# Expert FFN with routed tokens on one core: token ids stand behind the y rows in DRAM instead of in a tensor of their own

## What is computed

```python
def _L0_cond_ref(x, w, b):
    y = jax.lax.conv_general_dilated(x, w, window_strides=(1,), padding=[(K - 1, 0)], feature_group_count=D, ...)
    return y + b

def _L0_ffn_ref(x, w_router, w_experts):
    logits = jnp.einsum('bsh,eh->bse', x, w_router)
    idx = jnp.argmax(logits, axis=-1)
    all_out = jnp.einsum('bsh,efh->bsef', x, w_experts)
    out = jnp.take_along_axis(all_out, idx[:, :, None, None], axis=2)[:, :, 0, :]
    return out
x = x + _L0_ffn_ref(_L0_cond_ref(x, cond_2048[:, None, :], L0_cond_b), L0_ffn_w_router, L0_ffn_w_experts)
```

## Time and profile before

| | |
|---|---|
| median of 3 runs | 599.31 us |
| the profiled execution | 599.66 us |
| its span | 598.0 us |
| PE busy | 546.1 us (91%) |
| DVE busy | 348.2 us (58%) |
| ACT busy | 192.9 us (32%) |
| POOL busy | 221.2 us (37%) |
| mean granted TensorE clock | 0.957 |
| HBM read, written | 93.45 MB, 40.52 MB |

### The profile page before, as it was taken

One profiled execution on the slowest core, in us unless ns is written; L12 is line 12 of the kernel. 1 busy time (PEld: TensorE's weight loads), 2 busy tenths in 40 slices (PEclk: granted clock), 3 DMA queues, 4 the chain that ended last, 5 costly groups with the idle time before them and its releaser, 6 DMA issues.

```text
span 598.0 us, 10202 instructions
## 1 busy us (share of the span) xinstructions
PE 546.1 (91%) x3151; PEld 456.9 (76%) x3152; DVE 348.2 (58%) x404; ACT 192.9 (32%) x361; POOL 221.2 (37%) x222
## 2 busy tenths in 40 slices
PE   9999997789799987999899999999999999999930
PEld 7988886669688765788778888888888888888830
DVE  7999999449079561243887433275348332755720
ACT  7764654425390000012545110051015100514200
POOL 1300898765637722332222233321432242324321
PEclk9999999869999989799989999999999999999975
DMA  8734738626888359454998956368558754795451
GB/s 349 277 111 151 266 122 272 237 73 251 285 258 329 95 175 360 169 159 157 329 379 273 317 176 198 118 224 303 176 172 289 242 175 141 221 305 176 130 186 36
DMA packets 54936, 129.44 MB, mean 216 GB/s; under 512 B 7936, under 2 KB 29056, under 8 KB 54656
## 3 DMA queue, kind: packets, MB, share of 16 engines
q0 software_dynamic: 17616, 55.10, 26.3%
q1 hardware_dynamic: 15840, 54.42, 25.9%
q10 hardware_dynamic: 21456, 19.60, 12.0%
HBM read 93.45 MB, written 40.52 MB: 224 GB/s over the span
## 4 chain that ended last, share of the span: by engine, by line
PE 53%; DMA 4%; issue 2%; DVE 1%; ACT 1%; ACTq 1%; POOL 0%; POOLq 0%; DVEq 0%
PE ps L1099 53%; DMA out<-x_row,ids_first 2%; DMA x_row<-x_rows,idx 2%; ACT w_sb L522 1%; DMA out<-x_row,idx 1%; DVE w_sb L842 0%; ACTq L364 0%; POOL x_row L1183 0%; DVE x_row L870 0%; DVE ys L862 0%; DVE y_cols L857 0%; POOLq L1208 0%; DVEq L879 0%; DMA idx_in_sb<-id_sorted 0%; POOL idx L1214 0%
## 5 line engine op out<-in xcount | busy, mean ns | idle before, releaser
L1099 PE MATMUL ps<-w_sb,ys 128*128 128x512 f32 x1680 | 388.9, 394 | 11.2 <-DVE ys L862 6.3
L1099 PEld LDWEIGHTS ps<-w_sb,ys 128*128 128x128 f32 x1680 | 318.9, 190 | 80.1 <-issue 10.3
L857 DVE STREAM_TRANSPOSE y_cols<-y_blk 128x1024 f32<-128x1024 f32 x37 | 46.0, 1244 | 165.1 <-PE ps L1099 141.1
L541 ACT CAST ys<-y_cols 128x1024 fp32r<-128x1024 f32 x37 | 39.1, 1057 | 284.1 <-DVE y_cols L857 258.9
L684 DVE SCALAR_TENSOR_TENSOR y_pre<-x_all,cst,y_pre 128x1024 f32<-128x1024 f32 x72 | 87.3, 1288 | 0.1
L975 PE MATMUL ps<-x_all,bands 128*128 128x128 f32 x640 | 78.2, 279 | 4.0 <-issue 3.9
L975 PEld LDWEIGHTS ps<-x_all,bands 128*128 128x128 f32 x640 | 74.0, 193 | 7.5 <-issue 7.4
L842 DVE TENSOR_TENSOR w_sb<-w_raw,w_sb 128x1024 fp32r<-128x1024 f32 x56 | 64.2, 1220 | 20.2 <-ACT w_sb L522 17.3
L1190 POOL DMA_INDIRECT out<-x_row,idx x32 | 37.6, 1175 | 86.4 <-DVE x_row L870 80.9
L1214 POOL COPY idx<-idx_in_sb 128x1 int32<-128x1 int32 x34 | 9.3, 273 | 147.5 <-DMA out<-x_row,idx 136.4
L522 ACT CAST w_sb<-w_raw 128x1024 fp32r<-128x1024 f32 x56 | 53.9, 1048 | 21.5 <-PE ps L1099 15.5
(11 more groups left out here) (130 smaller groups left out, 208.7 us busy)
## 6 DMA issues: line engine op xcount, KB each, us to landing
w_raw<-experts SPq DMA_DIRECT2D x56, 512.0 KB
y_blk<-y_sorted ACTq DMA_DIRECT2D x148, 128.0 KB
x_all<-x_t SPq DMA_DIRECT2D x32, 520.0 KB, 6.0
w_lead<-experts SPq DMA_DIRECT2D x8, 512.0 KB
bands<-conv_full SPq DMA_DIRECT2D x2, 1024.0 KB, 10.9
y_blk<-y_sorted SPq DMA_DIRECT2D x8, 128.0 KB
idx_in_sb<-id_sorted POOLq DMA_DIRECT2D x36, 1.0 KB
x_row<-x_rows,idx POOLq DMA_INDIRECT x34
```

What stands on the lines that cost most here:

```text
L541: nc.scalar.copy(ys[:, HI, k, :, :].rearrange("p c s -> p (c s)"), y_cols[k][:, :, :].rearrange("p c s -> p (c s)")).then_inc(ys_hi, 1)
L857: V.transpose(y_cols[k][:, :, :].rearrange("p m (t i) -> p t m i", t=4), y_blk[:, k, :, :, :]).then_inc(y_blocks, 1)
L1099: mm = nc.tensor.matmul(out_ps[k][:, f * HALF:(f + 1) * HALF], ys[:, a, k, c, :], w_sb[:, (b * HC + c) * H + f * HALF:(b * HC + c) * H + ( ...
```

## The change

The tensor `id_sorted` is gone. A row of `y_sorted` has 1040 instead of 1024 elements (`ROW`), 4160 B: the 16 behind the row of y (`ID_COPIES`) hold the token's id. The staging buffers have the same rows, 512 B more per partition each. POOL writes the ids of a group into the staging buffer with one copy (`write_ids`), and the scatter of rows carries them along. The scatters of ids, `find_rest`, `fill_rest` and `fill_ids` are gone. Instead POOL writes 128 empty rows with the id `NO_TOKEN` to the start of each expert's part before the first group is scattered (`empty_rows`, eight direct DMAs out of one row per partition in `rows_odd`); the tokens' rows are then written over them. Waits on `id_out` become waits on `y_out`.

```diff
-        y_sorted = nc.dram_tensor("y_sorted", [EXPERTS * TOKENS, H], F32, kind="Internal").ap()
-        id_sorted = nc.dram_tensor("id_sorted", [ROWS, ID_STEP], I32, kind="Internal").ap()
+        y_sorted = nc.dram_tensor("y_sorted", [ROWS, ROW], F32, kind="Internal").ap()
...
                 if g == 1 and n == g * HC:
 
                     act.wait_ge(before_ready, 1)
+                    act.wait_ge(no_token_out, EXPERTS * 16)
...
             act.wait_ge(first_table, 1)
             act.wait_ge(y_out[1], 2 * TPG * 16)
-            act.wait_ge(rest_out, 32)
...
             low_y(1, 1)
-            find_rest()
             count_slots()
...
-            G.memset(no_token[:, :], NO_TOKEN).then_inc(no_token_ready, 1)
-            G.memset(token[:, TILES:], 0).then_inc(token_ready, 1)
-            G.tensor_copy(token[:, 0:TILES], const(C_TOKEN, TILES)).then_inc(token_ready, 1)
+            G.memset(empty_row[:, 0:H], 0.0).then_inc(no_token_ready, 1)
+            G.memset(empty_row[:, H:].bitcast(I32), NO_TOKEN).then_inc(no_token_ready, 1)
+            G.tensor_copy(token[:, :], const(C_TOKEN, TILES)).then_inc(token_ready, 1)
...
                 pool.wait_ge(turn_copied, (g + 1) * HC * 2)
                 pool.sem_inc(dma_allowed, 1)
+                pool.wait_ge(ids_written, g + 1)
...
+            def write_ids(g):
+
+                if g == 0:
+                    pool.wait_ge(token_ready, 1)
+                elif g == 1:
+
+                    pool.wait_ge(no_token_out, EXPERTS * 16)
+                else:
+
+                    pool.wait_ge(y_out[g % 2], TPG * 16)
                 pool.sem_inc(dma_allowed, 1)
...
+                ids = token[:, g * TPG:(g + 1) * TPG].unsqueeze(2).to_broadcast([P, TPG, ID_COPIES])
+                G.tensor_copy(rows_of(g)[:, :, H:].bitcast(I32), ids).then_inc(ids_written, 1)
+
+            def empty_rows():
+
+                pool.wait_ge(no_token_ready, 2)
+
+                pool.wait_ge(conv_mm, 2)
+                pool.sem_inc(dma_allowed, 1)
+                for e in range(EXPERTS):
+                    G.dma_start(y_sorted[e * TOKENS:e * TOKENS + P, :], empty_row).then_inc(no_token_out, 16)
...
-                G.dma_start(idx_in_sb[:, k, :], id_sorted[bass.ds(row, P), 0:2]).then_inc(idx_in[k], 16)
+                G.dma_start(idx_in_sb[:, k, :], y_sorted.bitcast(I32)[bass.ds(row, P), H:H + 2]).then_inc(idx_in[k], 16)
...
-            for g in range(LAST):
-                scatter_y(g)
-                scatter_ids(g)
+            empty_rows()
+            write_ids(0)
+            write_ids(1)
+            scatter_y(0)
+            write_ids(2)
+            scatter_y(1)
+            write_ids(3)
+            scatter_y(2)
 
             pool.wait_ge(first_known, 1)
-            pool.wait_ge(id_out, LAST * TPG * 16)
+            pool.wait_ge(y_out[0], 2 * TPG * 16)
+            pool.wait_ge(y_out[1], TPG * 16)
...
             scatter_y(LAST)
-            fill_rest()
-            scatter_ids(LAST)
-            fill_ids()
             scatter(0, 0, ids_first[:, 0, 0:1])
             pool.wait_ge(first_table, 1)
-            pool.wait_ge(id_out, GROUPS * TPG * 16)
-            pool.wait_ge(id_rest_out, 32)
+            pool.wait_ge(y_out[1], 2 * TPG * 16)
```

More of the change, by code:

```diff
@@ L103 @@
 SLOTS = LOOP + ROUNDS * RING + 3
-FILL = 8
-ID_STEP = 32
-FILL_PARTS = P // EXPERTS
+ID_COPIES = 16
+ROW = H + ID_COPIES
 C_IDENT = 0
@@ L115 @@
 C_NTH = C_EXPERT + EXPERTS
-C_OWN = C_NTH + EXPERTS
-C_PART = C_OWN + EXPERTS
-C_END = C_PART + 1
-C_SPLIT = C_END + 1
+C_SPLIT = C_NTH + EXPERTS
 C_SLOT = C_SPLIT + TILES
@@ L225, in build @@
         x_row = sb("x_row", [P, RING, H])
-        raw_at = slot_at + 32 * KB
+        sb("row_ends0", [P, TPG * ID_COPIES])
+        raw_at = slot_at + 4 * TPG * ROW
         w_raw = sb("w_raw", [P, HC, H])
-        x_at = raw_at + 32 * KB
+        sb("row_ends1", [P, TPG * ID_COPIES])
+        x_at = raw_at + 4 * TPG * ROW
         x_all = sb("x_all", [P, PE_RING + DVE_RING, X_LEN])
@@ L241, in build @@
         y_cols = [over(f"y_cols{k}", [P, HC, P], slot_at + 8 * KB + 4 * KB * k) for k in range(RING)]
-        stage = [over("rows_even", [P, TPG, H], slot_at), over("rows_odd", [P, TPG, H], raw_at)]
+        stage = [over("rows_even", [P, TPG, ROW], slot_at), over("rows_odd", [P, TPG, ROW], raw_at)]
         w_lead = over("w_lead", [P, HC, H], x_at)
@@ L250, in build @@
         assert 3 * (SLOTS - EARLY) * EXPERTS <= GT
+        empty_row = stage[1][:, TPG - 1, :]
         cst = sb("cst", [P, N_CONST])
@@ L254, in build @@
         before = sb("before", [P, 2 * P], BF16)
[L255 removed]
+        token = sb("token", [P, TILES], I32)
         top = sb("top", [P, TPG])
@@ L361, in load_y @@
         def load_y(queue, row, k):
-            src = y_sorted[bass.ds(row, P), :].rearrange("(t i) (q f) -> i q t f", t=4, q=4)
+            src = y_sorted[bass.ds(row, P), 0:H].rearrange("(t i) (q f) -> i q t f", t=4, q=4)
             for q in range(4):
@@ L760, in count_slots @@
                 step(V.tensor_reduce(n_of, many, AX.X, ALU.add))
-            def find_rest():
-                row, end, first_block = one[:, 8:9], const(C_END, 1), one[:, 10:11]
-                far = float(2 * ROWS)
-                step(V.tensor_tensor(tmp, base, const(C_OWN), ALU.mult))
-                step(V.tensor_reduce(row, tmp, AX.X, ALU.add))
-                step(V.tensor_scalar(one[:, 11:12], row, float(FILL - 1), None, ALU.add))
-                step(V.tensor_copy(fill_i[:, 2:3], one[:, 11:12]))
-                step(V.tensor_scalar(fill_i[:, 3:4], fill_i[:, 2:3], FILL.bit_length() - 1, None, ALU.logical_shift_right))
-                step(V.tensor_copy(first_block, fill_i[:, 3:4]))
-                step(V.tensor_scalar(one[:, 12:13], first_block, float(FILL), None, ALU.mult))
-                step(V.tensor_tensor(row, row, const(C_PART, 1), ALU.add))
-                step(V.tensor_tensor(one[:, 13:14], row, end, ALU.is_ge))
-                step(V.tensor_tensor(one[:, 12:13], row, one[:, 12:13], ALU.is_ge))
-                step(V.tensor_tensor(one[:, 12:13], one[:, 12:13], one[:, 13:14], ALU.max))
-                step(V.scalar_tensor_tensor(out=fill_i[:, 0:1], in0=one[:, 12:13], scalar=far, in1=row, op0=ALU.mult, op1=ALU.add))
-                step(V.tensor_tensor(first_block, first_block, const(C_PART, 1), ALU.add))
-                step(V.scalar_tensor_tensor(out=one[:, 14:15], in0=first_block, scalar=float(FILL), in1=end, op0=ALU.mult, op1=ALU.is_ge))
-                V.scalar_tensor_tensor(out=fill_i[:, 1:2], in0=one[:, 14:15], scalar=far, in1=first_block, op0=ALU.mult, op1=ALU.add
-                                       ).then_inc(fill_ready, 1)
             def order_experts():
@@ L1153, in scatter_y @@
                                          oob_is_err=False).then_inc(y_out[g % 2], 16)
-            def scatter_ids(g):
+            def write_ids(g):
                 if g == 0:
-                    pool.wait_ge(token_ready, 2)
-                    pool.sem_inc(dma_allowed, 1)
-                for j in range(TPG):
-                    n = g * TPG + j
-                    G.indirect_dma_start(id_sorted, at(pos_i[:, g, j:j + 1]), token[:, n:n + ID_STEP], None, bounds_check=last_row,
-                                         oob_is_err=False).then_inc(id_out, 16)
```

30 lines of the change are left out of this document (3 added, 27 removed).

## The result

The changed kernel took 571.09 us (median of 4 runs, 569.80 to 571.15), the kernel before beside it 598.63 us (4 runs, 595.94 to 601.25). The ratio is 0.9535, with a 95% interval from 0.9489 to 0.9581. That is 27.5 us of gain where 8.9 were forecast. The profiled execution took 571.02 us, its span is 569.4 us against 598.0.

The account below looks back on a forecast made before the run. TensorE sets the end from the expert stage on, so gaps ahead, from POOL's queue order, and the clock they cost count. Terms -7.7 and -1.2 sum to -8.9 us: 599.66 to 590.8, 590.4 against the median, written 590.5; range 581 to 600.

Parts of the forecast that it names:

- Group 2's y scatter waits for its positions before and after, so it stays: POOL, groups 0 to 2: dropping 24 id scatters of 1.28 us moves only the first id read and gathers; gain 0.
- a start of the expert stage that is unchanged: TensorE's first expert matmul: stays at 173.56 us; a start later than 175 would show the forecast wrong.
- rival B: TensorE's unreleased gaps, 100 to 132 and 155 to 164 us, go too: 7 to 10 us more, 578 to 585; chance 0.13.
- the wait for `x_row`: Ahead of block 5: earlier POOL output scatters remove the 5.09 us gap and 2.6 us of clock behind it, -7.7 us.
- the 1.22 us for `ys` ahead of block 3: VectorE without `find_rest` has the slot table and block 3's `ys` 2.8 us earlier, so this TensorE wait goes: -1.2 us.
- The empty rows: Eight direct DMAs on POOL, 4.26 MB, 12 us of DMA time: land by 45 us, hidden by some 15 us.
- The id copies: Four POOL copies of 128 elements beside the rows: 0 to 4.6 us each.
- The earlier gathers beside `w_lead`: At about 168 us, 1.5 MB beside the last four weight loads: cost 0 to 4.4 us, taken as 0.
- The row pitch: Rows of 4160 B, misaligned: block 3's load 0.5 us longer by the skill's rule, held by 1.7 us of slack; sum unchanged.
- TensorE's 2.26 us of gaps and 1.7 us of clock: Near block 3, gaps that nothing releases and the clock loss behind them: left as they are, bounds 0 to 3.9 us gain.
- C: Gain given back before the expert stage: gathers or later y rows delay or stretch block 0 by 3 to 6 us; 594 to 599; chance 0.22.
- D's hold: POOL instructions held during VectorE's unbroken work, 26 to 60 us; two holds show 16 us, giving 606, slower; chance 0.13.

Follow-up runs that it names:

- The kernels with dead scatters: Changed kernel with id scatters of groups 0 to 2 put back unread: 578.58 us (128 B), 579.31 (writing nothing), 577.68 (512 B); with POOL made late, 588.92 and 584.86.
- the repeat without the stall: The kernel before, unchanged, run and profiled once more on another chip: 591.01 us (10 runs, 586.51 to 593.94).

## Why the prediction was wrong

**The step that failed** is "Group 2's y scatter waits for its positions before and after, so it stays", and with it a start of the expert stage that is unchanged. On the profile of before the first half is true, but two things stood behind it. The places themselves came 15.3 us late (138.50 against 123.18), by the stall in 100 to 132 us that the earlier trace rows shows and that I left to rival B at 0.13; that is all of the 15.5 us of the measured pair. And where that stall is absent, POOL's queue is what holds y scatter 2 (131.67 against 124.20), because one long y scatter and 16 id scatters of 1.28 us or more stand ahead of it. The stall hid this second limit; reading one execution, I took the limit that ended last for the only one. The kernels with dead scatters show the queue's part as 6 to 8 us where POOL is late. Of the stall the repeats show that it comes with id scatters, on some chips, and goes with them; its cause is open. In the measured pair the forecast terms came as priced: 7.7 and 1.2, with 15.5 for the start and 3.9 for the gaps below, make 28.3 of the 28.6 us of span.

**The term that was priced on one execution** is the wait for `x_row`. The mechanism was right: the first output scatter stands right behind the y rows (177.64 after 176.37), and no wait for `ys` is left in that profile. I priced it at 5.09 + 2.6 us by a profile in which the stage had started late. In the repeat without the stall it is 10.5 + 1.9. And I had only half of the cause: the two transfers took 9 us each beside the weight load, which the kernel before issued 0.6 us behind the scatter of the earlier trace rows:

```profile
218.54 5.28 SPq L399 DMA_DIRECT2D w_raw<-experts  x8
```

I had read the 9.28 us as the scatter's own and even carried it over to the time after, where it was 4.6.

**Right:** the 1.22 us for `ys` ahead of block 3 are gone (forecast 1.2); put back alone, `find_rest` shows 0.58 us of wait, ahead of block 4, so its part in them is not shown. The wait for `x_row` does hang on the last group's twelve instructions: 9.36 us come back with them, and none with eight. The empty rows hidden: issued at 25.88 to 30.5, waited for until 44.62, 16 us ahead of the first y scatter. The id copies took 1.1 to 1.6 us each, in the bounds of 0 to 4.6. The earlier gathers beside `w_lead` leave no gap in block 0. The row pitch cost nothing that shows; the alignment rule of the Trainium skill ("DMA: Bandwidth & Descriptors", How a descriptor splits into AXI transactions) would by my estimate have made one load 0.5 us longer, and no run shows it.

**Not as foreseen:** TensorE's 2.26 us of gaps and 1.7 us of clock, left in the sum, went too (bounds 0 to 3.9, the full 3.9 came).

**The rivals.** B named the right stretches and gave 578 to 585; its cause, that the small writes hold the engines up, is neither shown nor refuted: scatters that write nothing cost the same, but on a chip without the stall, where the cost was POOL's queue. The measured 571 lies below B as well, since B kept the sum's other terms and put only 7 to 10 us on top. C didn't happen. D's hold (on a y scatter of group 0) came in both repeats of the changed kernel, 16.66 and 16.67 us long, and cost it nothing that can be seen: these executions took 572.37 and 570.89 us, the first profiled one, without a hold, 571.02. No direct DMA or copy ahead of 60 us was held.

## What to carry to other kernels

A profile shows the limit that ended last in that execution. Before a removed queue entry is costed at nothing because another wait covers it, ask when it would be ready if that other wait were gone, and whether an odd stall in the profile is that wait; the stall's own window deserves a repeat. When a transfer on the critical chain takes twice its usual time, look at what other load was issued in the same microseconds: moving one past the other can remove a wait that looks like a late queue. An instruction on a queue that feeds two waits (a landing and a later group) should be counted against both.

## What the runs showed of the hardware

One indirect scatter of 128 rows on POOL took 16.7 to 19.6 us in thirteen of the eighteen profiles in which POOL's order there was the usual one, always the fifth of group 0, from 69 us to 85.7 to 89.1 us; VectorE works without idle time all through this stretch, with 16 scalar_tensor_tensor operations in a row from 69.5 to 88 us. In the five profiles without it, the scatters in that stretch took 1.4 to 2.1 us each; many elsewhere take 0.97. The Trainium skill ("SBUF — State Buffer", SBUF: two separate sides) says that a VectorE operation with two SBUF inputs and a POOL operation that reads SBUF shut each other out for one instruction; here the scatter lasted over 14 to 16 such operations, and no run here shows the cause. A scatter whose rows are all out of range keeps POOL as long as one that writes, 0.97 us and 0.30 to the next. A scatter of 0.5 MB to `out` landed 4.4 to 4.6 us after its issue, and after 10.5 us beside a load of 4 MB. A semaphore raised by POOL behind eight scatters in the order of the code was there by 69.25 us, when four of them had run and the fifth started at 69.50. Where TensorE stood idle from 102.7 to 111.9 us, its granted clock was at the lower level (0.50) from 106 to 114 us and full again from 116.
